# A fused graph-convolution, Mamba-scan and LSTM kernel: broadcasts of B and C moved by half a slot, small operations moved from VectorE to GpSimd

## The reference

```
x = x + mamba(layernorm(relu(adj @ layernorm(x) @ gcn_w + gcn_b)))
x = x + lstm_part(layernorm(x))

mamba(h):
  xc, z = split(h @ w_in)                      # 256 channels each
  u     = silu(conv4(xc) + conv_b)             # causal, 4 taps
  dbc   = u @ w_xp                             # 8 for dt, 16 for B, 16 for C
  dt    = softplus(dbc[:, :8] @ w_dt + b_dt)
  for each of 16 states n, each token t:
    h[n] = exp(dt * A[n]) * h[n] + dt * B[n, t] * u
    y   += h[n] * C[n, t]
  return ((y + u * d_skip) * silu(z)) @ w_out
```

## Time and profile before

| | |
|---|---|
| median of 3 runs | 1697.48 us (1696.55 to 1701.78) |
| the profiled execution | 1698.79 us, span 1696.9 us |
| busy, share of the span | PE 92%, DVE 87%, POOL 61%, ACT 59% |
| steps 4 to 15 of the loop | about 299 to 1247 us of the span |
| drain | about 1247 to 1422 us |
| LSTM | about 1422 to 1686 us |

### The profile page before, as it was taken

The page is one execution under the profiler, slowest core; times in us unless marked ns, Lnnn a source line. Parts: engine busy times, 40 slices in busy tenths (PEclk is TensorE's granted clock), DMA queues, the critical chain, the costliest instruction groups (busy, mean ns, idle before and its releaser), DMA issues. The chain is left out here.

```text
span 1696.9 us, 21136 instructions
## 1 busy us (share of the span) xinstructions
PE 1556.1 (92%) x5282; PEld 791.8 (47%) x5282; DVE 1482.2 (87%) x1687; ACT 1005.5 (59%) x2093; POOL 1041.3 (61%) x471
## 2 busy tenths in 40 slices
PE   6999999999999999999999999999977677999994
PEld 2444344444444434343444444444422225999993
DVE  8416999999999999999999999999996995557998
ACT  2244666667575757576666667575757554555552
POOL 4024788887878778878788787878885651001221
PEclk9999999999999999999999999999988899999997
DMA  8976665757566666665665757566610202000002
GB/s 311 343 253 236 229 213 196 255 169 272 197 241 224 215 242 205 235 214 213 224 229 187 257 171 269 203 237 230 209 47 0 94 6 106 0 0 1 0 0 99
DMA packets 52073, 298.31 MB, mean 176 GB/s; under 512 B 5522, under 2 KB 5522, under 8 KB 19092
## 3 DMA queue, kind: packets, MB, share of 16 engines
q1 hardware_dynamic: 49680, 293.30, 48.8%
q10 hardware_dynamic: 2308, 4.20, 0.6%
HBM read 285.68 MB, written 11.80 MB: 175 GB/s over the span
## 5 line engine op out<-in xcount | busy, mean ns | idle before, releaser
L509 PE MATMUL bank<-ring,xh 128*128 128x512 f32 x2048 | 953.1, 593 | 15.5 <-DVE xh L989 15.0
L890 POOL TENSOR_TENSOR work<-work 128x1024 f32<-128x1024 f32 x210 | 516.6, 2460 | 238.3 <-DVE work L1081 232.0
L1123 DVE TENSOR_TENSOR_SCAN work<-bank,hstate,work 128x512 f32<-128x512 f32 x512 | 627.2, 1266 | 2.7 <-ACT bank L760 1.3
L509 PEld LDWEIGHTS bank<-ring,xh 128*128 128x128 f32 x2048 | 388.4, 190 | 458.3 <-issue 422.3
L760 ACT ACTIVATE bank<-work,a_neg 128x512 f32<-128x512 f32 x512 | 345.6, 688 | 306.2 <-DVE work L1123 305.9
L1073 DVE TENSOR_TENSOR work<-work,bank 128x1024 f32<-128x1024 f32 x256 | 309.5, 1214 | 60.0 <-PE bank L446 46.3
L446 PE MATMUL bank<-bc_parts,sel 96*128 96x512 bf16 x512 | 192.9, 385 | 33.3 <-DVE work L1081 25.8
L1081 DVE TENSOR_TENSOR work<-work,bank 128x1024 f32<-128x1024 f32 x182 | 216.2, 1194 | 0.0
L441 PE MATMUL bank<-work,w_sb 128*128 128x512 f32 (+2 forms) x352 | 183.5, 618 | 25.4 <-ACT work L676 11.2
L951 POOL TENSOR_TENSOR work<-work 128x256 f32 x32 | 28.5, 891 | 235.9 <-ACT work L797 235.9
L853 POOL TENSOR_TENSOR work<-work 128x1024 f32<-128x1024 f32 x48 | 113.3, 2361 | 79.9 <-ACT work L658 79.7
(11 more groups left out here) (148 smaller groups left out, 1581.4 us busy)
## 6 DMA issues: line engine op xcount, KB each, us to landing
ring<-adj_t SPq DMA_DIRECT2D x256, 1024.0 KB, 4.8
xh<-x_rows SPq DMA_DIRECT2D x16, 256.0 KB, 6.7
work<-x_t SPq DMA_DIRECT2D x16, 256.0 KB, 4.8
x_scratch<-work ACTq DMA_DIRECT2D x16, 256.0 KB, 5.4
work<-x_scratch SPq DMA_DIRECT2D x1, 4096.0 KB, 13.6
out_t<-work SPq DMA_DIRECT2D x16, 256.0 KB, 2.7
xl_scratch<-work SPq DMA_DIRECT2D x13, 256.0 KB, 2.2
ring<-xl_scratch SPq DMA_DIRECT2D x1, 3328.0 KB, 13.1
```

Source lines behind the costliest of these rows:

```text
L509: last = nc.tensor.matmul(mixed[:, :], xn[:, j, :], a, start=(j == 0), stop=(j == BLK - 1))
L890: nc.gpsimd.tensor_tensor(out=acc, in0=hc[0] if n == 1 else acc, in1=hc[n % 2], op=ALU.add).then_inc(y_added, 1)
L1123: nc.vector.tensor_tensor_scan(hb[s % 2][:, h, :], da[h], dbu[s % 2][:, h, :], hstate[:, HV * s + h:HV * s + h + 1], ALU.mult, ALU.add).th ...
```

## The change

SHARED puts z0 and z1 at 5.5 and 6.5 in place of 5 and 5.5. On PE the broadcast of B for state s+2 is at the middle of slot s, the first two of a chunk at the middles of slots 14 and 15 of the step before; the broadcast of C for state s-1 is at the head of slot s, and that of state 15 behind slot 15 (in the drain C stays at the middle). ACT reads z0 at slot 6 and z1 at slot 7, and makes its copies of C behind the exponentials and save_state. r1 is on POOL, as are all three steps of dt in the drain's step 16; on POOL these stand ahead of the slot's add, with dtu behind the add of slot 13. The sum is now (relu - rem) and then + log. SP's store of xl is at piece 6. In the drain the post list is delayed from slot 12 on, and xl is made behind the last slot.

```diff
@@ -68,7 +68,7 @@
...
 SHARED = [("gcn", 0, "pre"), ("cen", 1, "pre"), ("var", 2, "pre"), ("xc0", 4, "pre"), ("xc1", 4.5, "pre"),
-          ("z0", 5, "pre"), ("z1", 5.5, "pre"), ("dbc", 9, "pre"), ("dt0", 10, "pre"), ("dt1", 10.5, "pre"),
+          ("z0", 5.5, "pre"), ("z1", 6.5, "pre"), ("dbc", 9, "pre"), ("dt0", 10, "pre"), ("dt1", 10.5, "pre"),
           ("out", 11.5, "post"), ("pcen", 12.5, "post"), ("pvar", 13.5, "post")]
...
@@ -95,7 +95,7 @@
...
-    late = dict(pre=8, post=16)[stage]
+    late = dict(pre=8, post=12)[stage]
     if not drains(k) or s < late:
...
@@ -356,7 +356,7 @@
...
                         r = j % RING
-                        if j == 2 and not (isinstance(k, int) and k < 4):
+                        if j == 6 and not (isinstance(k, int) and k < 4):
                             sp.wait_ge(xl_ready, k - 3)
...
@@ -441,10 +441,10 @@
...
-                def spread(bank_, ready, row, n):
+                def spread(bank_, ready, row, n, rows=bc_parts[par]):
                     nc.tensor.matmul(bank_[n % 2][:, :], sel[:, row * P:(row + 1) * P],
-                                     bc_parts[par][:, :], start=True, stop=True).then_inc(ready, 1)
+                                     rows[:, :], start=True, stop=True).then_inc(ready, 1)
...
@@ -455,14 +455,24 @@
...
-                def spread_b(n):
-                    wait(pe, dbu_done, DS * cs + (n - 1))
-                    spread(b_bank, b_ready, n, n)
+                def spread_b(s):
+                    if s < DS - 2 and scan:
+                        wait(pe, dbu_done, DS * cs + (s + 1))
+                        spread(b_bank, b_ready, s + 2, s)
+                    if s >= DS - 2 and pre:
+                        n = s - (DS - 2)
+                        if n == 0:
+                            pe.wait_ge(low_ready, k)
+                            pe.wait_ge(mid_ready, k)
+                        wait(pe, dbu_done, DS * (k - 1) + (n - 1))
+                        spread(b_bank, b_ready, n, n, bc_parts[1 - par])
...
                     shared_steps(s, 0.5)
-                    if scan and s > 0:
+                    if scan and s > 0 and drains(k):
                         spread_c(s)
+                    spread_b(s)
...
@@ -483,14 +493,9 @@
...
                 for s in range(16):
-                    if scan and s == 0:
-                        pe.wait_ge(low_ready, cs + 1)
-                        pe.wait_ge(mid_ready, cs + 1)
-                        spread_b(0)
-                    if scan and s < DS - 1:
-                        spread_b(s + 1)
-                    if scan and s == 0:
+                    if scan and not drains(k) and s >= 1:
+                        spread_c(s - 1)
+                    if drains(k) and scan and s == 0:
                         spread_c(0)
...
@@ -514,6 +519,8 @@
...
                             state_sum(s - 2, cs)
+                if scan and not drains(k):
+                    spread_c(DS - 1)
...
@@ -669,11 +676,12 @@
...
                         nc.scalar.activation(xc[1 - q][:, :, 0:HALO], xc[q][:, :, CH:CH + HALO], ACT.Copy).then_inc(halo_ready, 1)
-                        if post:
+                    if s in (6, 7):
+                        h = s - 6
+                        if post and h == 0:
                             act.wait_ge(y_ready, k - 2)
-                        for h in range(HV):
-                            written(f"z{h}")
-                            nc.scalar.activation(sz[q][:, h, :], shared[:, :], ACT.Copy).then_inc(shared_read, 1)
+                        written(f"z{h}")
+                        nc.scalar.activation(sz[q][:, h, :], shared[:, :], ACT.Copy).then_inc(shared_read, 1)
                     if s == 6:
...
@@ -743,7 +751,7 @@
...
                 for s in range(16):
-                    if scan and s >= 1 and (drains(k) or s - 1 in POOL_HC):
+                    if scan and s >= 1 and drains(k):
                         copy_c(s - 1)
...
@@ -763,6 +771,8 @@
...
                             save_state(cs - 1, DS - 1)
+                    if scan and not drains(k) and s - 1 in POOL_HC:
+                        copy_c(s - 1)
                     if pre:
...
@@ -853,20 +863,23 @@
...
                 def pre_part(s):
-                    if drains(k):
-                        return
+                    if s == 10:
+                        pool.wait_ge(high_ready, k)
+                        nc.gpsimd.tensor_tensor(out=r1[0:PARTS * BC, :], in0=dbc[0:PARTS * BC, :], in1=bc_parts[q][:, :],
+                                                op=ALU.subtract).then_inc(r1_ready, 1)
                     if s == 12:
-                        pool.wait_ge(log_dt, k)
+                        pool.wait_ge(pos_dt, HV * k)
                         pool.wait_ge(rem_dt, k)
-                        nc.gpsimd.tensor_tensor(out=wb, in0=wd, in1=wb, op=ALU.subtract).then_inc(sum_dt, 1)
+                        nc.gpsimd.tensor_tensor(out=wa, in0=wa, in1=wb, op=ALU.subtract).then_inc(sum_dt, 1)
                     if s == 13:
                         pool.wait_ge(sum_dt, k)
-                        pool.wait_ge(pos_dt, HV * k)
-                        nc.gpsimd.tensor_tensor(out=dt[q], in0=wa, in1=wb, op=ALU.add).then_inc(dt_ready, 1)
-                    if s == 14:
-                        pool.wait_ge(dt_ready, k)
-                        nc.gpsimd.tensor_tensor(out=dtu[q], in0=dt[q], in1=u[q], op=ALU.mult).then_inc(dtu_ready, 1)
+                        pool.wait_ge(log_dt, k)
+                        nc.gpsimd.tensor_tensor(out=dt[q], in0=wa, in1=wd, op=ALU.add).then_inc(dt_ready, 1)
+                def make_dtu():
+                    pool.wait_ge(dt_ready, k)
+                    nc.gpsimd.tensor_tensor(out=dtu[q], in0=dt[q], in1=u[q], op=ALU.mult).then_inc(dtu_ready, 1)
...
@@ -877,7 +890,7 @@
...
                         nc.gpsimd.tensor_tensor(out=by_step(yp), in0=by_token(yv), in1=by_token(sz[q]), op=ALU.mult).then_inc(y_ready, 1)
-                    if s == 15 and not (isinstance(k, int) and k == NC + 2):
+                    if s == 15:
                         make_xl(pool, nc.gpsimd, k)
...
@@ -922,16 +935,20 @@
...
                         add_tap(s)
+                    if pre:
+                        pre_part(planned(k, s, "pre"))
                     if scan and drains(k):
...
                         add(s - 1)
-                    if pre:
-                        pre_part(s)
+                    if pre and planned(k, s, "pre") == 13:
+                        make_dtu()
                     if post and s > 0:
...
                     add(DS - 1)
+                if post and drains(k) and k < NC + 2:
+                    make_xl(pool, nc.gpsimd, k)
...
@@ -1010,8 +1027,6 @@
...
                             finish_y()
-                        if pre and s in (12, 13, 14):
-                            make_dt(s)
                     if post and t == 12:
...
@@ -1020,11 +1035,7 @@
...
                         nc.vector.tensor_tensor(out=ht, in0=ht, in1=shared[:, :], op=ALU.mult).then_inc(shared_read, 1)
-                    if pre and s == 10:
-                        dve.wait_ge(high_ready, k)
-                        nc.vector.tensor_tensor(out=r1[0:PARTS * BC, :], in0=dbc[0:PARTS * BC, :], in1=bc_parts[q][:, :],
-                                                op=ALU.subtract).then_inc(r1_ready, 1)
-                    if pre and s == 12 and not drains(k):
+                    if pre and s == 12:
                         dve.wait_ge(one_dt, k)
...
@@ -1047,22 +1058,6 @@
...
                     nc.vector.tensor_tensor(out=by_step(yp), in0=by_token(yv), in1=by_token(sz[q]), op=ALU.mult).then_inc(y_ready, 1)
-                def make_dt(s):
-                    if s == 12:
-                        dve.wait_ge(log_dt, k)
-                        nc.vector.scalar_tensor_tensor(out=wb, in0=wc, scalar=-1.0, in1=wb, op0=ALU.add,
-                                                       op1=ALU.subtract).then_inc(rem_dt, 1)
-                        dve.wait_ge(rem_dt, k)
-                        nc.vector.tensor_tensor(out=wb, in0=wd, in1=wb, op=ALU.subtract).then_inc(sum_dt, 1)
-                    if s == 13:
-                        dve.wait_ge(sum_dt, k)
-                        dve.wait_ge(pos_dt, HV * k)
-                        nc.vector.tensor_tensor(out=dt[q], in0=wa, in1=wb, op=ALU.add).then_inc(dt_ready, 1)
-                    if s == 14:
-                        dve.wait_ge(dt_ready, k)
-                        nc.vector.tensor_tensor(out=dtu[q], in0=dt[q], in1=u[q], op=ALU.mult).then_inc(dtu_ready, 1)
...
```

## The result

| | before | after |
|---|---|---|
| median, beside each other | 1697.01 us (1696.3 to 1701.78) | 1690.49 us (1688.01 to 1692.9) |
| profiled execution | 1698.79, span 1696.9 | 1688.01, span 1686.2 |
| after / before | | 0.9955 [0.9941, 0.997] |

The account below looks back on a forecast made before the run. PE and DVE, of nearly equal length, were taken to bound each other. Saving 1.05 us in each of 14 chunks (15) plus 8 in the drain took 1698.8 to 1675.8, said as 1674; range 1642 to 1692.

Parts of the forecast that it names:

- (f): SP's xl store at piece 6: PE sees about 0.1 us, counted as 0; cover is four pieces in the ring.
- (e): Dt work ahead of GpSimd's adds: 0.35 us chunk-start wait goes every other chunk (mean 0.17); 1.13 us at turns stays.
- `out` as the bound: PE's chain to `out` paces steady chunks: DVE's x1c sum waits 2.4 us, only 1.1 of 3.5 saved stays.
- Rival 1: PE follows as fast as DVE asks: a chunk saves 3.8 us, the time is 1636; chance 0.18.
- rem behind add(10): In each steady chunk DVE's L1029 stands behind GpSimd's add of state 10: 2.05 us, 0.9 of 1.1 saved stays.
- (g): Three ScalarE copies of C behind the exponentials: one delays xc1, costing 0.54 us on PE's phase.
- rival 2: L1029 always waits for a whole GpSimd operation, 3.4 us; chunk back at about 79.4, time 1690; chance 0.2.
- (d): Difference L1025 moved from DVE to GpSimd: DVE loses 1.87 us; it takes 1.3 in GpSimd's idle time, costing 0.
- (a): B broadcast half a slot earlier: PE gets about 2 us more lead, DVE's 1.63 us wait in slot 5 goes.
- (c): z0 and z1 at 5.5 and 6.5: PE's 0.63 us wait and 0.17 restart go, 0.80 off its chain.
- (b): C broadcast half a slot later: still early for DVE's product; PE's wait for the state product 2 us shorter.
- the drain: Chunks after the steady stretch: 6.5 us saved plus 1.5 in the very last; together 8, bounds 0 and 14.

Follow-up runs that it names:

- experiment 1: Changed kernel with only SP's xl store back at piece 2: 1681.42 us, 0.9891 of the kernel before.
- 2: Kernel before with only the xl store moved to piece 6: 1711.6 us, 1.007 of the kernel before.
- experiment 3: Changed kernel, store still at piece 6, four steps in the loop's body, 2 turns instead of 5: 1682.69 us, 0.9904 of before.
- experiment 4: Changed kernel with the xl store at piece 2 and `out` at the head of slot 11: 1653.03 us, 0.9727 of before.
- experiment 5: Changed kernel with the xl store at piece 2 and r1 back on DVE: 1662.49 us, 0.9784 of before.
- 6: Changed kernel with the xl store at piece 2, `out` at the head of slot 11 and r1 back on DVE: 1661.68 us, 0.9784 of before.
- experiment 9: Changed kernel with the xl store at piece 2, z0 and z1 back at 5 and 5.5, read together in slot 5: 1696.94 us, 0.9993 of before.
- experiment 10: Kernel of experiment 4 with ACT's copies of C ahead of the exponentials again: 1679.56 us, 0.989 of before.
- experiment 12: Kernel of experiment 4 with four steps in the loop's body: 1645.14 us, 0.9689 of before.

## Why the prediction missed, step by step

**(f), the xl store: wrong, and it is most of the miss.** The step that failed is this term of the sum. "I count 0; the cover is four pieces in the ring" looked at who uses the data and not at who else uses the DMA engines. It was put at 0, and measures 9 to 11 us within the change and 12 alone. **(e)'s "DVE idles 1.13 us in the loop's turn, which stays"** is the same error seen from DVE: it became 3.15. In the five turn chunks 4.5 us were to be gained and 8.6 were lost, 13 in all; experiment 1 gets 10.3 of these back. Experiments 1, 2 and 3 each show it from another side. The rest of the miss is rem's term, below: with (f) undone the kernel is at 1681, still 7 us above the 1674 forecast, and its steady chunks gain 8.6 us of the 15. The Trainium skill ("Runtime: NRT & Kernel Launch", section "Instruction fetch mechanics") says that a taken branch whose target is not already at hand forces a DMA fetch before execution goes on; the trace agrees, queue 14 has four or five packets in the 14 us around the turn, and D0 follows 2.1 us behind one of them. That such packets come late when bulk loads are in flight, 3.8 us apart instead of 2, is what the runs add.

What was not tried: holding the loads with a wait alone while the store stays at piece 6. So it is shown by experiment that the store's place decides; that the gap in the loads does it, and not something else about the store, rests on the packet records and on the turn's 1.13 us in both kernels that have that gap.

**`out` as the bound: right.** x1c came 36.19 us after D4 (36.4 forecast), with 0.84 to xc1 (0.90) and 33.23 from there to `out` (33.5). It waited 1.37 for PE and 0.42 at a scan for an exponential, 1.8 where I had 2.4. Rival 1, that PE follows DVE, is out as the change stands; experiment 4 shows that 28 us lay behind that one place in SHARED.

**rem behind add(10): right in kind, too low in size, and its meaning missed.** Forecast 2.05, measured 2.85: rem started 36.8 us after D4 as against 37.0, but add(10) started at 36.2 and not 35.6, 0.6 ahead of it instead of 1.4, and so had more still to run. Rem ended at D4 + 39.57, forecast 39.05, before 39.93: of the 0.9 us that this stretch was to save, 0.4 came, and 0.5 us in 14 chunks is about what is missing without (f). Of add(10)'s 0.6 us, 0.35 are hc(10)'s wait ahead of it. Its row names a DVE scan, but the scan that it needs had ended at 1141.74; what it also needs is ACT's copy of C(10), which (g) puts behind the exponentials (at 1143.10 before):

```profile
1144.90 0.59 ACT L745 ACTIVATE work<-bank 128x512 f32<-128x512 f32 x1
```

That the chunk without a turn came within 0.1 of the forecast is in part luck: such chunks were 79.14 long before and not 79.2, and each gets dtu's whole 0.35, where I took the mean of 0.17. The rule cited from "SBUF — State Buffer" of the Trainium skill agrees with every run: rem takes 1.22 us with GpSimd idle, 1.50 and 1.60 when it starts ahead of the add and behind hc(10), with the add at 3.14, and 2.85 when it starts behind the add; its end is always 1.1 us after that of the operation it stood behind. I had it as a danger in rival 2 ("DVE 1.4 us earlier, or GpSimd 1.4 us later"), 0.8 of which came true.

**(d), r1 on GpSimd: the working held, the edit was priced at the wrong engine.** It takes 1.15 us there (1.3 forecast) and costs GpSimd nothing. But I booked its 1.87 us as gain up to where `out` bounds, and took them for work, though 1.3 of them are a wait for GpSimd (experiment 5). With `out` the bound, it gains nothing, and by moving GpSimd's chain ahead of rem it loses 1.3 us a chunk; it cost 19 us (experiment 1 against 5), and brought 8.7 with `out` early (4 against 6). The forecast compared one chunk of before and after, where (a), (c) and (d) are all in, and never asked what each is worth with the others present.

**(a) and (c): right.** From slot 5's scans to slot 6's it was 6.35 us and is 4.62; experiment 9 gives (c) 0.9 us a chunk by itself. I had 0.8.

**(b): right.** PE's waits for the state product in this stretch (58.2 us in 74 waits) are gone; 21.6 in 23 for the input product have come. No DVE product waits for C.

**(g): wrongly accounted.** The 0.54 us on PE's phase came (D4 to xc1 went from 0.36 to 0.84), but experiment 10 shows what it buys: 26.5 us. (b) without (g) would have been a loss, and the prediction gave no price for that. It also set GpSimd's hc(10), and so add(10), 0.35 us back, as above: the prediction looked at what (g) does to PE and not to GpSimd.

**(e) and the drain: near, but not firm.** dtu ends 4.4 us ahead of D0. The drain and the rest gave 9.8 us for 8 in this trace; with the same drain, experiment 1's trace gives 6.4 and experiment 3's 5.0, with a wait for B of 6.26 in experiment 1 where this one has 3.94. Its rows answer to the earlier trace rows: B's two waits and x1c's 5.43 are gone, in their place

```profile
1306.19 1.22 DVE L1068 TENSOR_TENSOR work<-work,bank 128x1024 f32<-128x1024 f32 x1 [3.94 <-PE bank L446]
...
1326.03 2.35 DVE L1068 TENSOR_TENSOR work<-work,bank 128x1024 f32<-128x1024 f32 x2 [3.20 <-POOL work L882]
...
1390.15 2.46 DVE L1118 TENSOR_TENSOR_SCAN work<-bank,hstate,work 128x512 f32<-128x512 f32 x2 [1.59 <-POOL work L918]
```

a wait for B ahead of x1c, dtu 3.2 us late (about 4 forecast), and in the very last chunk a scan held by GpSimd's state product, so that 0.2 us was won there and not 1.5.

**The chances.** A price of zero for (f) had no range around it. Its effect can be had from the trace of before: the loads' gap around 1094 and the five waits for "issue" in the same place were both there, and so were queue 14's packets, alone in that gap; asking what else uses the DMA engines then could have given this rival.

## What to carry to other kernels

When a transfer is moved, list what shares its queues and its DMA engines at that moment, instruction fetch at a loop's turn among it: here that moved 9 to 12 us, though no data was late. Before taking an operation off an engine, find what bounds its next meeting point; if that is another engine, the saving is nothing, and the earlier start only changes who goes first in later collisions. Two edits that must go together, like a later broadcast and the copy that reads it, are priced together.

## What the runs showed of the hardware that was not expected

- At a turn of the hardware loop DVE stands 1.13 to 1.3 us in the kernel before and in experiment 1, where the last three 8 KB packets of queue 14 run alone on the DMA engines, and 3.15 to 3.8 us where they run among the `adj` loads; there ACT stands up to 4.1 (no wait of this kind before), and PE 2.57 behind ACT. By the times of kernels with three turns fewer, a turn costs 2.6 to 2.9 us (experiment 3) and 2.1 to 2.6 (experiment 12).
- The same SCALAR_TENSOR_TENSOR of 128x1024 takes 1.22 us with GpSimd idle, and else ends 1.1 us after the end of the GpSimd operation that was running at its start: 1.50 to 1.60 us behind hc(10), 2.85 behind add(10). Which of the two it is turns on 0.6 us. Moving a GpSimd add by one slot is worth 1.3% of the kernel.
- The difference of 96x512 with a bf16 input takes 1.15 us on GpSimd, and on DVE 0.66 at its shortest and 1.95 in the steady chunk (experiment 5). It too starts behind a GpSimd operation there, and ends 0.55 us after it in every steady chunk.
